# Adding softmax weights of two key blocks on GpSimd before the product with ones, and moving the normalisation's transfers

## The chip, the cores and the metric

The kernel runs on one core of a Trainium2 chip. The metric is the time of one execution on the device in microseconds (us). The core has a matrix engine (TensorE, PE in the profile), VectorE (DVE), ScalarE (ACT), GpSimd (POOL) and SyncE (SP); each works through its own instruction list in order, and semaphores tie the lists together. SP issues most of the DMA transfers, POOL some.

## The reference, cut to what matters

```python
h = layernorm(x) * (1 + ca) + sa
q, k, v = projections of layernorm(h), 16 heads of 32; q, k rotated, then layernormed per head
scores = einsum('bhqd,bhkd->bhqk', q, k) / sqrt(32)
scores = where(causal, scores, min)
w = softmax(scores, axis=-1)
x = x + ga * (einsum('bhqk,bhkd->bhqd', w, v) @ Wo + bo)
x = x + gb * gated_ffn(layernorm(x) * (1 + cb) + sb)
```

Batch 4, 1024 positions, width 512, all in float32. Only the softmax and the product with V are touched here.

## The kernel before, in words

Four stages run one after the other: `qkv_stage`, `attention_stage` (L578), `project_stage`, `ffn_stage`. The change lies in `attention_stage` alone.

It works on 16 groups of four heads. Each engine's list is written out in steps `k`; a unit `n` is 12 consecutive steps, `w` is the step in the unit. In unit n the engines do, side by side: the scores of group n in natural orientation to find each row's maximum (`score` on PE L791, `peak` on DVE L877); the preparation of group n+1 in w=1 and w=3 (`prepare` on PE L782: eight transposes; `widen` on ACT L946; `high` on POOL L750: the part that float32r holds; `low` on DVE L872: the rest, `whole` minus `halves`, both in SBUF), after which SP copies the halves of four heads into `stack` (`lay_stacks`, L700, 12 transfers); and, 14 steps behind the scores, the softmax of a group by blocks: `BLOCKS` are the 12 pairs of a half of the queries and a block of 128 keys, with widths 512, 384, 256, 128 for the first half and 512 five times, 384, 256, 128 for the second.

For a block, `shift` (PE L812) makes scores minus maximum, transposed, for each of four heads, in one of two PSUM buffers (`psB`); `exponent` (ACT L953) writes `probT`; a step later `weigh` (PE L827) multiplies the four heads' `probT` with V into `psO`, and then again with a matrix of ones into `psL`, which gives the sums of the softmax. In step w, block w-2 is shifted and block w-3 weighed. After the last block of a half, `take` on DVE (L906) and ACT (L968) move `psO` and `psL` out.

The maxima: `gather` (DVE L894) makes a table from them at the end of w=11, with L897, L899, L902 and L904 in a row, each waiting for the one before; `turn_peaks` (PE L807) transposes it in w=0, ahead of that step's `weigh`; ACT copies it and SP lays it into the stack.

`normalise` (POOL L757) divides by the sums: they go out to DRAM (L759), come back as 128x32 (`few`, L761), DVE takes the reciprocal (L937), they go out again (L763) and come back over all partitions (L766, four transfers), and POOL multiplies (L769). POOL's queue issues these transfers and waits for each. SP's list in a unit: peaks in w=0, `load` and all 12 stack transfers in w=4, V in w=5, the store of group n-2 in w=10.

PE's order in a step is: shifts of heads 0 and 1, two score items, shifts of heads 2 and 3, then the transposes of a preparation or of the peaks where there are any, then `weigh` with V and with ones. A score item waits for the maximum of the item two before (two slots of `psA`).

## Time and profile before

| | us |
|---|---|
| median of 3 runs (lowest, highest) | 2434.78 (2433.34, 2436.04) |
| the profiled execution | 2436.47 |
| its span, first to last instruction | 2434.3 |
| PE, DVE, ACT, POOL busy | 2242.7, 1200.8, 792.2, 728.7 |
| attention stage, from its first load to its last store | 400 to 1208 |

Times in rows are us from the start of the span; a row of the timeline has start, duration, engine, line, operation, tile written <- tiles read, shape, and in brackets the idle time before it and what ended it. "PEld" is the load of weights into the matrix engine, "PE" the product itself; SPq and POOLq are instructions of a queue. Products are pipelined, so the start of the next one says more than the duration.

### The profile page before, as it was taken

The numbers are of one execution on the slowest core, as the hardware profiler recorded it, in microseconds if no ns is written. First come the engines' busy times: TensorE is split into PE (matmuls) and PEld (weight loads), VectorE is DVE, ScalarE is ACT, GpSimd is POOL, SyncE is SP. The second block draws the span as 40 slices with busy tenths as digits, with TensorE's granted clock in tenths as the row PEclk, the third lists the DMA queues.
The fourth block names the chain that finished last, engine by engine and source line by source line (L and its number), as shares of the span: only waits on it lengthen the run. The fifth ranks groups of instructions, "written<-read, shape, count | busy, mean of one in ns | idle before, by whom it ended". The sixth has DMA issues, their size and how long they took to land. (4 is left out here: it accounts for less than half of the span.)

```text
span 2434.3 us, 32672 instructions
## 1 busy us (share of the span) xinstructions
PE 2242.7 (92%) x12008; PEld 1649.6 (68%) x12008; DVE 1200.8 (49%) x2775; ACT 792.2 (33%) x1671; POOL 728.7 (30%) x694
## 2 busy tenths in 40 slices
PE   6999993799999999999678799999999999999998
PEld 3777771455555555555356588888888888888887
DVE  5999995566665665665279512222222222221212
ACT  3333331155555555555445411111111111111111
POOL 2677775002112112111277122222222222222221
PEclk8999996599999999999899899999999999999999
DMA  6222223555465465452288411212121211111111
GB/s 225 70 96 94 103 87 120 118 134 132 102 152 126 107 151 130 107 128 76 68 256 303 161 52 52 70 48 69 52 69 49 66 56 65 52 64 37 52 53 52
DMA packets 161834, 243.71 MB, mean 100 GB/s; under 512 B 17124, under 2 KB 84292, under 8 KB 161184
## 3 DMA queue, kind: packets, MB, share of 16 engines
q1 hardware_dynamic: 153184, 220.66, 31.0%
q0 software_dynamic: 7456, 18.07, 2.6%
q10 hardware_dynamic: 1056, 3.15, 0.3%
q8 instruction: 87, 1.43, 0.2%
q14 instruction: 51, 0.42, 0.1%
HBM read 131.69 MB, written 59.26 MB: 78 GB/s over the span
## 5 line engine op out<-in xcount | busy, mean ns | idle before, releaser
L1324 DVE TENSOR_TENSOR f_gu<-f_psU,f_silu 128x512 f32<-128x512 f32 x128 | 88.6, 692 | 712.3 <-PE f_psU L1391 712.3
L961 ACT ACTIVATE b_probT<-b_psB 128x512 f32<-128x512 f32 (+3 forms) x768 | 339.4, 490 | 300.0 <-PE b_psB L824 220.9
L891 DVE TENSOR_REDUCE b_top<-b_psA 128x2 f32<-128x1024 f32 (+2 forms) x320 | 288.6, 902 | 134.0 <-PE b_psA L803 133.8
L1280 POOL TENSOR_SCALAR f_wd_hi<-f_wd 128x512 fp32r<-128x512 f32 x128 | 83.4, 652 | 819.7 <-PE f_psD L1376 775.9
L821 PE MATMUL b_psB<-b_stack 98*128 98x512 f32 (+3 forms) x768 | 273.6, 401 | 5.1 <-ACT b_probT L961 4.6
L821 PEld LDWEIGHTS b_psB<-b_stack 98*128 98x128 f32 x768 | 141.4, 189 | 156.0 <-issue 103.2
L1300 ACT ACTIVATE f_silu<-f_psG 128x512 f32<-128x512 f32 x128 | 76.5, 598 | 504.2 <-PE f_psG L1391 504.2
L803 PE MATMUL b_psA<-b_stack 96*128 96x512 f32 (+3 forms) x768 | 193.5, 373 | 35.8 <-DMA b_stack<-b_halves 20.1
L1389 PE MATMUL f_psG<-f_hT_hi,w_hi 128*128 128x512 f32 x512 | 200.4, 391 | 11.0 <-DVE f_hT_lo L1318 11.0
L1391 PE MATMUL f_psG<-f_hT_lo,w_hi 128*128 128x512 f32 x512 | 199.9, 390 | 0.0
L1390 PE MATMUL f_psG<-f_hT_hi,w_lo 128*128 128x512 f32 x512 | 199.9, 390 | 0.0
L1295 ACT ACTIVATE f_gu_hi<-f_gu 128x512 fp32r<-128x512 f32 x128 | 80.9, 632 | 364.5 <-DVE f_gu L1324 364.5
L1390 PE MATMUL f_psU<-f_hT_hi,w_lo 128*128 128x512 f32 x512 | 199.2, 389 | 0.0
L1391 PE MATMUL f_psU<-f_hT_lo,w_hi 128*128 128x512 f32 x512 | 199.2, 389 | 0.0
L1389 PE MATMUL f_psU<-f_hT_hi,w_hi 128*128 128x512 f32 x512 | 199.2, 389 | 0.0
L1374 PE MATMUL f_psD<-f_wd_hi,f_gu_hi 128*128 128x512 f32 x512 | 199.2, 389 | 0.0
L1375 PE MATMUL f_psD<-f_wd_lo,f_gu_hi 128*128 128x512 f32 x512 | 199.2, 389 | 0.0
L1376 PE MATMUL f_psD<-f_wd_hi,f_gu_lo 128*128 128x512 f32 x512 | 199.2, 389 | 0.0
L803 PEld LDWEIGHTS b_psA<-b_stack 96*128 96x128 f32 x768 | 136.2, 200 | 65.9 <-issue 22.6
L1282 POOL TENSOR_TENSOR f_wd_lo<-f_wd,f_wd_hi 128x512 fp32r<-128x512 f32 x128 | 168.8, 1319 | 10.7
L839 PE MATMUL b_psO<-b_probT,b_v 128*32 128x512 f32 (+3 forms) x1536 | 165.4, 503 | 0.0
L839 PE MATMUL b_psL<-b_probT,b_ones 128*32 128x512 f32 (+3 forms) x1536 | 159.0, 486 | 0.0
(178 smaller groups left out, 4084.4 us busy)
## 6 DMA issues: line engine op xcount, KB each, us to landing
b_stack<-b_halves SPq DMA_DIRECT2D x192, 256.0 KB, 5.1
f_wd<-in_wd_t SPq DMA_DIRECT2D x128, 256.0 KB, 2.6
qkv_d<-a_t SPq DMA_DIRECT2D x32, 512.0 KB, 2.7
b_land<-qkv_d SPq DMA_DIRECT2D x32, 512.0 KB, 4.7
a_x<-in_x SPq DMA_DIRECT2D x32, 256.0 KB, 3.3
qkv_d<-a_v SPq DMA_DIRECT2D x32, 256.0 KB, 3.1
b_v<-qkv_d SPq DMA_DIRECT2D x16, 512.0 KB, 5.8
att_d<-b_att SPq DMA_DIRECT2D x16, 512.0 KB, 3.2
```

The lines of the kernel that those rows point to most:

```text
L803: mm = pe.matmul(out[:, h, 0:hi - lo], stack[0:ROWS, n % BUFS, 1, j, t * P:(t + 1) * P], stack[0:ROWS, n % BUFS, 0, j, lo:hi], start=True, ...
L821: mm = pe.matmul(psB[:, i % 2, cols], stack[0:NR, n % BUFS, 0, j, kb * P:(kb + 1) * P], stack[0:NR, n % BUFS, 1, j, first * P:(half + 1) * ...
L839: mm = pe.matmul(out[rows, (first - half * HALF) * P:W], ones[:] if summing else v[:, n % 2, kb, rows], probT[:, (NW * n + w) % 3, j, 0:(h ...
L891: last = dve.tensor_reduce(into, tile[:, :, 0:width], AX.X, ALU.max, negate=True)
L961: act.activation(probT[:, (NW * n + w) % 3, j, 0:width], psB[:, i % 2, 0:width], ACT.Exp).then_inc(s["expd"], 1)
L1282: pool.tensor_tensor(wd_lo[:, u % 2], wd[:, u % 2], wd_hi[:, u % 2].bitcast(F32), ALU.subtract).then_inc(s["wd_lo"], 1)
L1374: pe.matmul(out_t, gu_hi[:, u % 2, cols], wd_hi[:, u % 2], start=first, stop=False)
L1375: pe.matmul(out_t, gu_hi[:, u % 2, cols], wd_lo[:, u % 2], start=False, stop=False)
L1376: mm = pe.matmul(out_t, gu_lo[:, u % 2, cols], wd_hi[:, u % 2], start=False, stop=end)
L1389: pe.matmul(out_c, w_hi[:, m, k, cols], hi, start=(k == 0), stop=False)
L1390: pe.matmul(out_c, w_lo[:, m, k, cols], hi, start=False, stop=False)
L1391: mm = pe.matmul(out_c, w_hi[:, m, k, cols], lo, start=False, stop=(k == KC - 1))
```

## The change

It does four things. (1) `add_pair` on POOL adds the exponents of two neighbouring key blocks in place, head by head (four additions per pair, as wide as the second block), and PE multiplies with ones once per pair (`add_up`), three steps after the pair's second shift, in even steps only. (2) `probT` has five buffers in place of three. (3) SP lays the stack of one head (three transfers) per step, in w=4 to 7. (4) The transfers of the normalisation move from POOL's list to SP's, in w=6, 7, 9 and 10; DVE takes the reciprocal in w=8 as before, POOL multiplies in two halves in w=11, and the store goes to w=2 of the next unit.

```diff
...
     BUFS = 3
+    PROBS = 5
 
...
         return (at[0], BLOCKS[at[1]][0]) if at and BLOCKS[at[1]][1] == (BLOCKS[at[1]][0] + 1) * HALF - 1 else None
+
+    def pair_at(k):
+        at = shift_at(k)
+        return (at[0], at[1] // 2) if at and at[1] % 2 == 1 else None
+
+    def sum_at(k):
+        return pair_at(k - 3)
+
+    def take_sum_at(k):
+        return take_at(k - 2)
 
...
         peak_rows = sb("b_peak_rows", [8 * TB, P])
-        probT = sb("b_probT", [P, 3, 4, W])
+        probT = sb("b_probT", [P, PROBS, 4, W])
         sums = sb("b_sums", [P, 2, C])
...
 
-            def lay_stacks(n):
-                at_least(sp, s["shifted"], 4 * NW * (n - BUFS + 1))
-                sp.wait_ge(s["lo_done"], 2 * n + 2)
-                for j in range(4):
-                    for r, pair in enumerate((slice(0, 4, 3), slice(2, 4), slice(0, 2))):
-                        sp.dma_start(stack[r * HD:(r + 1) * HD, n % BUFS, :, j].bitcast(F32),
-                                     halves[j * HD:(j + 1) * HD, pair].bitcast(F32)).then_inc(stack_in[j], 16)
+            def lay_stacks(n, j):
+                if j == 0:
+                    at_least(sp, s["shifted"], 4 * NW * (n - BUFS + 1))
+                    sp.wait_ge(s["lo_done"], 2 * n + 2)
+                for r, pair in enumerate((slice(0, 4, 3), slice(2, 4), slice(0, 2))):
+                    sp.dma_start(stack[r * HD:(r + 1) * HD, n % BUFS, :, j].bitcast(F32),
+                                 halves[j * HD:(j + 1) * HD, pair].bitcast(F32)).then_inc(stack_in[j], 16)
 
...
                 sp.dma_start(dst, att[:, n % 2].rearrange("p (t q) -> p t q", q=P)).then_inc(stored, 16)
+
+            def sums_out(n):
+                sp.wait_ge(s["taken_l"], 2 * n + 2)
+                sp.dma_start(scratch["sums"][0], sums[0:P:HD, n % 2]).then_inc(s["sums_out"], 16)
+
+            def few_in(n):
+                sp.wait_ge(s["sums_out"], 16 * n + 16)
+                sp.dma_start(few[:, 0], scratch["sums"][0].rearrange("j (a c) -> (j a) c", c=C // HD)).then_inc(s["few_in"], 16)
+
+            def few_out(n):
+                sp.wait_ge(s["inverted"], n + 1)
+                sp.dma_start(scratch["sums"][1].rearrange("j (a c) -> (j a) c", c=C // HD), few[:, 1]).then_inc(s["few_out"], 16)
+
+            def wide_in(n):
+                sp.wait_ge(s["few_out"], 16 * n + 16)
+                for j in range(4):
+                    sp.dma_start(sums[j * HD:(j + 1) * HD, n % 2], scratch["sums"][1, j:j + 1].broadcast_to([HD, C])).then_inc(s["wide_in"], 16)
 
...
                     load(n + 2)
-                if w == 4 and n + 1 < NG:
-                    lay_stacks(n + 1)
-                if w == 5 and 0 <= n < NG:
+                if 0 <= n - 2 < NG - 1 and w in (6, 7, 9, 10):
+                    {6: sums_out, 7: few_in, 9: few_out, 10: wide_in}[w](n - 2)
+                if 4 <= w < 8 and n + 1 < NG:
+                    lay_stacks(n + 1, w - 4)
+                if w == 7 and 0 <= n < NG:
                     load_v(n)
-                if w == 10 and 0 <= n - 2 < NG:
-                    store(n - 2)
+                if w == 2 and 0 <= n - 3 < NG:
+                    store(n - 3)
             sp.wait_ge(stored, 16 * NG)
...
 
+            def add_pair(n, i):
+                half, kb = BLOCKS[2 * i + 1]
+                width = (half + 1) * W - max(kb, half * HALF) * P
+                at = (NW * n + 2 * i) % PROBS
+                whole_at = (half + 1) * W - max(kb - 1, half * HALF) * P
+                pool.wait_ge(s["weighed"], NW * n + 2 * i + 1)
+                for j in range(4):
+                    into = probT[:, at, j, whole_at - width:whole_at]
+                    pool.wait_ge(s["expd"], 4 * (NW * n + 2 * i + 1) + j + 1)
+                    add = pool.tensor_tensor(into, into, probT[:, (at + 1) % PROBS, j, 0:width], ALU.add)
+                add.then_inc(s["added"], 1)
+
             def normalise(n):
-                pool.wait_ge(s["taken_l"], 2 * n + 2)
-                pool.dma_start(scratch["sums"][0], sums[0:P:HD, n % 2]).then_inc(s["sums_out"], 16)
-                pool.wait_ge(s["sums_out"], 16 * n + 16)
-                pool.dma_start(few[:, 0], scratch["sums"][0].rearrange("j (a c) -> (j a) c", c=C // HD)).then_inc(s["few_in"], 16)
-                pool.wait_ge(s["inverted"], n + 1)
-                pool.dma_start(scratch["sums"][1].rearrange("j (a c) -> (j a) c", c=C // HD), few[:, 1]).then_inc(s["few_out"], 16)
-                pool.wait_ge(s["few_out"], 16 * n + 16)
-                for j in range(4):
-                    pool.dma_start(sums[j * HD:(j + 1) * HD, n % 2], scratch["sums"][1, j:j + 1].broadcast_to([HD, C])).then_inc(s["wide_in"], 16)
                 pool.wait_ge(s["wide_in"], 64 * n + 64)
                 pool.wait_ge(s["taken_o"], 2 * n + 2)
-                pool.tensor_tensor(att[:, n % 2], att[:, n % 2], sums[:, n % 2], ALU.mult).then_inc(s["scaled"], 1)
+                for half in range(2):
+                    cols = slice(half * W, (half + 1) * W)
+                    mul = pool.tensor_tensor(att[:, n % 2, cols], att[:, n % 2, cols], sums[:, n % 2, cols], ALU.mult)
+                mul.then_inc(s["scaled"], 1)
 
...
                     high(*prep_at(k))
-                at = take_at(k)
-                if at and at[1] == 1 and at[0] < NG - 1:
-                    normalise(at[0])
+                if pair_at(k):
+                    add_pair(*pair_at(k))
+                n, w = unit(k)
+                if w == 11 and 0 <= n - 2 < NG - 1:
+                    normalise(n - 2)
 
...
 
-            def weigh(n, w, summing):
+            def weigh(n, w):
                 half, kb = BLOCKS[w]
-                if not summing:
-                    pe.wait_ge(s["expd"], 4 * (NW * n + w) + 4)
-                    if w == 0:
-                        pe.wait_ge(s["v_in"], 16 * n + 16)
+                pe.wait_ge(s["expd"], 4 * (NW * n + w) + 4)
+                if w == 0:
+                    pe.wait_ge(s["v_in"], 16 * n + 16)
                 if kb == 0:
-                    at_least(pe, s["taken_l" if summing else "taken_o"], 2 * n + half)
+                    at_least(pe, s["taken_o"], 2 * n + half)
                 first = max(kb, half * HALF)
-                out = psL if summing else psO
                 for j in range(4):
                     rows = slice(j * HD, (j + 1) * HD)
-                    mm = pe.matmul(out[rows, (first - half * HALF) * P:W], ones[:] if summing else v[:, n % 2, kb, rows],
-                                   probT[:, (NW * n + w) % 3, j, 0:(half + 1) * W - first * P],
+                    mm = pe.matmul(psO[rows, (first - half * HALF) * P:W], v[:, n % 2, kb, rows],
+                                   probT[:, (NW * n + w) % PROBS, j, 0:(half + 1) * W - first * P],
                                    start=(kb == 0), stop=(kb == (half + 1) * HALF - 1), skip_group_check=True)
-                mm.then_inc(s["summed" if summing else "weighed"], 1)
+                mm.then_inc(s["weighed"], 1)
+
+            def add_up(n, i):
+                half, kb = BLOCKS[2 * i]
+                pe.wait_ge(s["added"], NW // 2 * n + i + 1)
+                if kb == 0:
+                    at_least(pe, s["taken_l"], 2 * n + half)
+                first = max(kb, half * HALF)
+                for j in range(4):
+                    mm = pe.matmul(psL[j * HD:(j + 1) * HD, (first - half * HALF) * P:W], ones[:],
+                                   probT[:, (NW * n + 2 * i) % PROBS, j, 0:(half + 1) * W - first * P],
+                                   start=(kb == 0), stop=(kb == (half + 1) * HALF - 2), skip_group_check=True)
+                mm.then_inc(s["summed"], 1)
 
...
                 if weigh_at(k):
-                    weigh(*weigh_at(k), False)
-                    weigh(*weigh_at(k), True)
+                    weigh(*weigh_at(k))
+                if sum_at(k):
+                    add_up(*sum_at(k))
 
...
                     low(*prep_at(k))
-                at = take_at(k - 5)
-                if at and at[1] == 1 and at[0] < NG - 1:
-                    dve.wait_ge(s["few_in"], 16 * at[0] + 16)
+                n, w = unit(k)
+                if w == 8 and 0 <= n - 2 < NG - 1:
+                    dve.wait_ge(s["few_in"], 16 * (n - 2) + 16)
                     dve.reciprocal(few[:, 1], few[:, 0]).then_inc(s["inverted"], 1)
-                at = take_at(k)
+                at = take_sum_at(k)
                 if at and at[0] == NG - 1:
...
                 if j == 0:
-                    at_least(act, s["summed"], NW * n + w - 2)
-                    at_least(act, s["weighed"], NW * n + w - 2)
+                    before = NW * n + w - PROBS
+                    if before % 2 == 0:
+                        at_least(act, s["summed"], before // 2 + 1)
+                    else:
+                        at_least(act, s["added"], before // 2 + 1)
+                        at_least(act, s["weighed"], before + 1)
                 width = (half + 1) * W - max(kb, half * HALF) * P
-                act.activation(probT[:, (NW * n + w) % 3, j, 0:width], psB[:, i % 2, 0:width], ACT.Exp).then_inc(s["expd"], 1)
+                act.activation(probT[:, (NW * n + w) % PROBS, j, 0:width], psB[:, i % 2, 0:width], ACT.Exp).then_inc(s["expd"], 1)
 
...
             def take(n, half):
-                act.wait_ge(s["summed"], NW * n + (HALF if half == 0 else NW))
+                act.wait_ge(s["summed"], (NW * n + (HALF if half == 0 else NW)) // 2)
                 at_least(act, s["scaled"], n - 1)
...
                         exponent(*shift_at(k), j)
-                    if j == 1 and take_at(k):
-                        take(*take_at(k))
+                    if j == 1 and take_sum_at(k):
+                        take(*take_sum_at(k))
                 if prep_at(k):
...
```

## Rows read from the trace of the kernel before

**Rows 1.** The page, busy time of the engines: us, share of the span, instructions.

```profile
PE 2242.7 (92%) x12008; PEld 1649.6 (68%) x12008; DVE 1200.8 (49%) x2775; ACT 792.2 (33%) x1671; POOL 728.7 (30%) x694
```

**Rows 2.** Busy time in a stretch: PE, PEld, DVE, ACT, POOL, clock, DMA share, GB/s.

```profile
616.00:664.00 48.00, 46.22 (x362) 27.71 (x360) 30.89 (x98) 26.37 (x57) 8.13 (x10) 1.00 0.51 123
```

**Rows 3.** The timeline, transposition of the peaks in w=0 of two units.

```profile
699.64 0.14 PEld L810 LDWEIGHTS b_psA<-b_ident,b_peaks 128*128 128x128 f32 x1
...
745.34 0.14 PEld L810 LDWEIGHTS b_psA<-b_ident,b_peaks 128*128 128x128 f32 x1
```

**Rows 4.** The timeline, step w=8 and the start of w=9, PE alone.

```profile
727.57 0.73 PE L821 MATMUL b_psB<-b_stack 98*128 98x512 f32 x2
...
729.67 1.06 PE L839 MATMUL b_psO<-b_probT,b_v 128*32 128x512 f32 x8
...
730.56 1.04 PE L839 MATMUL b_psL<-b_probT,b_ones 128*32 128x512 f32 x8
...
731.53 0.50 PE L821 MATMUL b_psB<-b_stack 98*128 98x512 f32 x1
```

**Rows 5.** The timeline, the two preparations in w=1 and w=3.

```profile
703.69 1.06 PE L788 MATMUL b_psA<-b_ident,b_land 128*128 128x128 f32 x8 [0.44 <-DVE b_top L891]
...
707.23 1.22 DVE L875 TENSOR_TENSOR b_halves<-b_whole,b_halves 128x1024 fp32r<-128x1024 f32 x1 [2.39 <-POOL b_halves L755]
...
714.27 1.05 POOL L755 TENSOR_SCALAR b_halves<-b_whole 128x1024 fp32r<-128x1024 f32 x1 [7.08 <-ACT b_whole L950]
...
715.35 1.23 DVE L875 TENSOR_TENSOR b_halves<-b_whole,b_halves 128x1024 fp32r<-128x1024 f32 x1 [2.86 <-POOL b_halves L755]
```

**Rows 6.** The timeline, start of w=1, and ones at width 256 with the next step.

```profile
701.33 0.33 PE L821 MATMUL b_psB<-b_stack 98*128 98x128 f32 x1
...
720.39 0.61 PE L839 MATMUL b_psL<-b_probT,b_ones 128*32 128x256 f32 x8
...
720.93 0.73 PE L821 MATMUL b_psB<-b_stack 98*128 98x512 f32 x2
```

**Rows 7.** The timeline, w=11, the gather of the peaks and the start of w=0.

```profile
739.69 0.44 PE L821 MATMUL b_psB<-b_stack 98*128 98x384 f32 x1
...
742.80 1.04 PE L839 MATMUL b_psL<-b_probT,b_ones 128*32 128x512 f32 x8
743.58 0.19 DVE L897 TENSOR_TENSOR b_least<-b_top 128x32 f32<-128x32 f32 x1
...
743.77 0.39 PE L821 MATMUL b_psB<-b_stack 98*128 98x256 f32 x1
...
744.25 0.19 DVE L904 TENSOR_TENSOR b_peaks<-b_least,b_peaks 128x32 fp32r<-128x32 f32 x1
```

**Rows 8.** Groups by line and shape: busy us, mean ns, idle before and its releaser.

```profile
L769 POOL TENSOR_TENSOR b_att<-b_att,b_sums 128x1024 f32<-128x1024 f32 x15 | 35.7, 2382 | 39.5 <-DMA b_sums<-sums_d 39.5
L273 POOL TENSOR_TENSOR a_h<-a_h,mod 128x512 f32<-128x512 f32 x32 | 41.0, 1280 | 0.0
```

**Rows 9.** The timeline, DVE beside POOL in the first and third stage.

```profile
75.42 1.92 POOL L281 TENSOR_TENSOR a_t<-a_t,a_hmean 128x1024 f32<-128x1024 f32 x1
...
76.56 0.81 DVE L407 TENSOR_SCALAR a_den<-a_vsum,a_ms2h 128x32 f32<-128x32 f32 x1
...
1235.00 1.28 POOL L1094 TENSOR_TENSOR w_lo<-p_wland,w_hi 128x512 fp32r<-128x512 f32 x1
1235.15 1.69 DVE L1150 TENSOR_TENSOR p_x<-p_gated,p_x 128x512 f32<-128x512 f32 x1
...
1240.55 0.69 DVE L1150 TENSOR_TENSOR p_x<-p_gated,p_x 128x512 f32<-128x512 f32 x1
```

**Rows 10.** Stacks seven to nine; landing of L759 (sums) and L761 (few), 568 to 1144.

```profile
723.94 3.37 SPq L705 DMA_DIRECT2D b_stack<-b_halves  x3
...
DMA to landing us min/median/max: 1.9/3.1/7.1
...
DMA to landing us min/median/max: 1.9/3.9/5.4
```

More of the change, by code:

```diff
@@ L665, in attention_stage @@
         names = ("mask_in ln_ready whole ident_ready consts k_ones qk_in v_in turned hi_done lo_done scored maxed peaks_ready "
-                 "peaks_turned peaks_copied peaks_in shifted expd weighed summed taken_o taken_l sums_out few_in inverted few_out "
+                 "peaks_turned peaks_copied peaks_in shifted expd weighed added summed taken_o taken_l sums_out few_in inverted few_out "
                  "wide_in scaled end_inverted end_scaled").split()
```

## The prediction

> **What bounds the kernel now.** I read the page's totals first: TensorE (PE) is busy for 92% of the span, VectorE (DVE) for 49%, GpSimd (POOL) for 30% [rows 1]. The change touches only the attention stage, so the table by stretches comes next: in 48 us of its middle PE is busy for 46.22 at a granted clock of 1.00 (the 2.4 GHz level), DVE for 30.89, ScalarE (ACT) for 26.37 and POOL for 8.13 [rows 2]. PE looks like the bound with a lot of free POOL beside it. That is an average, so I looked at one unit (12 steps, w = 0 to 11) step by step in the timeline. The transposition of the peaks, once per unit in w=0, starts at 699.64 and again at 745.34 [rows 3]: a unit takes 45.70 us, and 15 of them make up most of the stage.
>
> Two kinds of steps are to be seen. In w=7 to 11, PE sets the pace: step w=8 starts at 727.57, the products with V at 729.67, those with ones at 730.56, the next step at 731.53 [rows 4]. The 2.10 us before V are a ping-pong with ACT through two PSUM buffers (the third and fourth shift wait for exponents); 0.89 us are V, 0.97 us ones. In w=1 to 3, a chain sets the pace: transposes on PE at 703.69, ACT's widening, POOL's high part, DVE's low part at 707.23, then the maxima, scores and transposes queued behind it, and once more high at 714.27 and low at 715.35 [rows 5]. DVE stood idle for 2.39 and 2.86 us before its low parts, for POOL's high part, and PE's products with ones lie beside that chain at no cost. After it, DVE has maxima to catch up until w=6.
>
> **The products with ones.** A set costs 0.97 us at width 512 [rows 4] and 0.54 at 256 (720.39 to 720.93 [rows 6]), so 0.43 per 256 columns: 0.76 at 384 and 0.33 at 128. A unit has 6, 2, 2 and 2 of these: 5.82 + 1.52 + 1.08 + 0.66 = 9.08 us. Afterwards six sets are left, all in even steps: 4 x 0.97 + 2 x 0.54 = 4.96. So 4.12 us of PE work per unit go, 66 us in 16 units. What of it shows is a sum along the path, from the end of the second low part (T0 = 715.35 + 1.23 = 716.58 [rows 5]):
> - T0 to w=11: 23.11 us now (739.69 [rows 7]). w=4 to 6 win nothing: DVE's queued maxima set them, and w=6 gets a 512 set for a 128 one. w=7 and w=9 lose their sets of 512: 0.89 each, not 0.97, since V's set then bears the drain before the next step. w=8 has 256 in place of 512, 0.43. w=10 is unchanged. 23.11 - 0.89 - 0.43 - 0.89 = 20.9.
> - w=11: 4.08 - 0.89 = 3.19, and from there 1.57 to the peaks (743.77 to 745.34 [rows 3, 7]): 4.76 in place of 5.65.
> - Peaks to w=1: 1.69 (699.64 to 701.33 [rows 3, 6]), plus 0.21 for 512 in place of 384: 1.90.
> - w=1 to T0: 15.25 now (701.33 to 716.58 [rows 5, 6]), the chain: nothing won there, and the 512 set that w=2 gets lies beside it.
> Without any new wait a unit would take 20.9 + 4.76 + 1.90 + 15.25 = 42.8 us, 2.9 less.
>
> **What POOL takes over.** Its tensor_tensor takes 2382 ns for 1024 columns and 1280 ns for 512 [rows 8], so about 2.15 ns per column and 0.18 fixed: 1.0 us at 384 and 0.46 at 128. Per unit there are 4 x (1.0 + 0.46 + 1.28 + 1.28 + 1.0 + 0.46) = 22 us of additions, 2.6 for the scaling in halves and 2.1 for the two high parts: 27 of 43 us. Each pair is needed three steps later (some 9 us) and takes at most 5.1, so as an engine POOL isn't the bound, and its high parts come before the additions of their step.
>
> **What those additions do to DVE** is where I leave the intended sum. In the stage after attention, DVE's L1150 reads two SBUF tiles of 512 columns. When it is first (1240.55) it takes 0.69; started at 1235.15, 0.15 us behind a POOL operation that ran until 1236.28, it took 1.69 and ended 0.56 us after POOL did [rows 9]. A tensor_scalar of 128x32 (L407) took 0.81 us and ended at 77.37, right behind POOL's 75.42 + 1.92 = 77.34 [rows 9]. So such a DVE operation waits for the POOL operation under way. Before, POOL was mostly idle in attention; now three places meet:
> - First low part (two SBUF operands, 707.23, woken by the high part's end): behind that high part POOL's next instruction is an addition of 128 columns, its operands long ready. I take POOL as first: until 707.65, then DVE's 1.1 us of columns: +0.3 us on the chain.
> - Second low part, the same with 384 columns: 715.32 + 1.02, then 1.1: +0.9 us.
> - The gather of the peaks: L897, L899, L902, L904, 0.19 each, at 743.58 to 744.44, from 3.89 us after the start of w=11 [rows 7]. POOL's additions of pair 4 wait for block 8's product with V, which ends 3.11 us after that same start (742.80), so they run from about 3.25 to 7.35, four in a row. Each gather operation waits for its own predecessor, and meanwhile POOL has started its next: they end with additions 1, 2, 3, 4, at 7.35 in place of 4.75. The peaks' transposition stands in PE's queue ahead of V and ones; its turn now comes at 4.76, so all of it is stall: 7.45 in place of 4.76, +2.7 us.
> The bounds of each: nothing if DVE gets in first, and one whole addition per operation above; I take what the order of the two queues gives.
> No row shows the cast L902 beside POOL; the nearest is L407, which was held. The Trainium skill, "SBUF — State Buffer", section "Who interferes with whom", says that copies and casts can take the shared port pair as well as operations with two SBUF inputs; by that all four wait, while with a free cast the gather would end one addition (1.0 us) earlier. The nearest row alone gives the same choice.
>
> Unit: 20.9 + 7.45 + 1.90 + 15.25 + 1.2 = 46.7 us, **1.0 us longer than now**.
>
> **Normalisation on SyncE's queue (SP).** The reciprocal on DVE in w=8 now waits for a transfer that left POOL's queue for SP's. SP issues six stack transfers from T0 on (the seventh now starts at 723.94), then the sums, three more stacks (now 723.94 + 3.37 = 727.31, so 727.9 with the sums before them), then `few`, 128x32. With the medians of POOL's transfers (sums 3.1, `few` 3.9) it lands at 727.9 + 3.9 = 731.8, T0 + 15.2; with the slowest (7.1 and 5.4) at 723.94 + 12.5 = 736.4, T0 + 19.8 [rows 10]. From landing to w=11: reciprocal 0.35, maxima of w=9 1.23 + 0.84, scores to the third shift 0.45, the rest of w=10 2.76 (this unit's own spacing), together 5.6. Behind the wait stand the maxima of w=9, and for those PE's scores of w=10. So it costs nothing up to T0 + 15.3, and beyond, 1 us per us. I take 15.2, the medians: nothing, with thin cover. The later steps (four broadcasts, scaling on POOL) have some 3 us to spare before the next high part; POOL loses seven issues and their waits, SP gets them. Nothing waits behind SP's other new places: the stacks are needed 12 us later, V's tile later still. The Trainium skill, "DMA: Bandwidth & Descriptors", section "Queues, rings and completion order", has each DMA engine take one ring's descriptors in order; by that `few` waits behind the stacks issued before it; the sum stays if that wait fits into the 3.9 us, and each us more would be one of C. No row here shows it.
>
> **The sum.** Units 2 to 14: 13 x 1.0 = +13.0. Unit 1 (first low part free): +0.7. Unit 15 (no low parts, so all odd steps win; gather held): -1.1. The last unit has no scores, wins 3 and pays 2 at the end for four last additions and their set: -1. Total +11.6. The profiled execution took 2436.47 us (span 2434.3), 1.7 above the median of the runs, 2434.78. Against that median: **2446 us**.
>
> **Rivals.**
> A, the forecast, 0.50: own range 2434 to 2460.
> B, the gather slips through (faster), 0.22: if the additions are over or not yet begun when DVE gathers, the 2.7 us go and a unit takes 44.0; with free low parts as well 42.8. 15 units: 25 to 43 us off, 2392 to 2410. It decides at one point, whether a POOL addition runs 3.9 us after w=11 starts. For it: PE's 66 us of removed work are real. Against: both sides hang on the same PE step.
> C, `few` lands late and DVE stands in w=8 (slower still), 0.20: with a landing at T0 + 17.3, about midway between the two ends, +2 us in 13 units: 2472. For: twelve stacks fill that stretch, and the sums once took 7.1. Against: the medians.
> D, only part of the gather is held, or one low part gets in first, 0.08: about 0.9 us less per unit: 2434.
>
> **Numbers.** Differences under 0.2% (4.9 us) can't be told from none for this kernel. Below 2408 lies about a tenth (the better half of B), above 2478 less than a tenth (C beyond its middle). Faster: B and a sliver of A and D, 0.25; same: D and the lower edge of A, 0.09; slower 0.66.
>
> **What would show it.** The transpositions of the peaks 46 to 47 us apart; L897 to L904 taking some 0.3 to 1.0 us each and ending with POOL's additions; PE idle before L810's counterpart, released by DVE's peaks; the second low part near 2 us in place of 1.23; products with ones 80 to 90 us busy in place of 159; no idle DVE before the reciprocal. The forecast is wrong if the gather keeps 0.19 per operation (B), or if the reciprocal waits for `few` (C).

## The result, and the profile after

After: 2497.03 us, median of 4 runs (2494.32 to 2499.82); before, beside it, 2434.15 (2433.34 to 2436.04). The ratio is 1.0253, 95% interval 1.0240 to 1.0266: slower, as forecast, but by 63 us in place of some 11, and outside the range of 2434 to 2460. The profiled execution took 2494.82 us, its span is 2492.8 (before 2434.3).

The page of the kernel after, its busy times (us, share of the span, instructions), to be held against [rows 1]:

```profile
PE 2241.2 (90%) x11240; PEld 1644.5 (66%) x11240; DVE 1250.1 (50%) x2775; ACT 793.5 (32%) x1671; POOL 1040.3 (42%) x988
```

768 products fewer, and PE is as long busy as before (2242.7): what is left of its work runs slower. POOL has 312 us more, DVE 49 us more with the same number of instructions.

The timeline of the kernel after, one unit: the transposition of the peaks at both ends, the start of w=1, both low parts, the start of w=11 ([rows 3, 5, 6, 7] before):

```profile
723.54 0.18 PEld L848 LDWEIGHTS b_psA<-b_ident,b_peaks 128*128 128x128 f32 x1 [3.13 <-DVE b_peaks L953]
...
726.98 0.33 PE L859 MATMUL b_psB<-b_stack 98*128 98x128 f32 x1
...
732.88 1.48 DVE L924 TENSOR_TENSOR b_halves<-b_whole,b_halves 128x1024 fp32r<-128x1024 f32 x1 [2.40 <-POOL b_halves L785]
...
741.25 2.02 DVE L924 TENSOR_TENSOR b_halves<-b_whole,b_halves 128x1024 fp32r<-128x1024 f32 x1 [2.86 <-POOL b_halves L785]
...
764.36 0.44 PE L859 MATMUL b_psB<-b_stack 98*128 98x384 f32 x1
...
772.20 0.18 PEld L848 LDWEIGHTS b_psA<-b_ident,b_peaks 128*128 128x128 f32 x1 [3.12 <-DVE b_peaks L953]
```

This unit takes 48.66 us, one of three so short; the other ten between 520.06 and 1174.35 take 50.5 to 51.3 us, and the mean is (1174.35 - 520.06) / 13 = 50.33, against 45.70 in [rows 3]. In front of each transposition PE now stands idle for some 3.1 us and waits for DVE's table of the peaks. Why that is late, the same timeline shows a few us earlier:

```profile
767.76 3.86 POOL L796 TENSOR_TENSOR b_probT<-b_probT 128x384 f32<-128x384 f32 x4 [2.39 <-PE b_psO L875]
...
768.25 0.57 DVE L946 TENSOR_TENSOR b_least<-b_top 128x32 f32<-128x32 f32 x1
...
768.85 0.92 DVE L948 SCALAR_TENSOR_TENSOR b_least<-b_corner,b_least 128x32 f32<-128x32 f32 x1
769.80 0.90 DVE L951 CAST b_peaks<-b_least 128x32 fp32r<-128x32 f32 x1
770.74 0.92 DVE L953 TENSOR_TENSOR b_peaks<-b_least,b_peaks 128x32 fp32r<-128x32 f32 x1
771.58 2.50 POOL L804 TENSOR_TENSOR b_att<-b_att,b_sums 128x512 f32<-128x512 f32 x2
```

Four operations of 0.19 us each [rows 7] take 0.57 to 0.92 and end one by one with POOL's four additions (0.965 us each from 767.76). The cast is among them, as the Trainium skill ("SBUF — State Buffer", "Who interferes with whom") allows for casts: it takes 0.90 us here and 0.18 with POOL idle. DVE's work on the maxima, which reads PSUM, isn't held: between 468 and 1270 us its reductions of 128x1024 take 1219 ns on average, 1223 in the kernel before. The 49 us that DVE gained lie in the gather and in the low parts.

What I had not looked for stands in the column of the granted clock, behind the five columns of busy time. The table by stretches of the kernel after, behind the transposition at 772.20, then behind the second preparation of two units (columns as in [rows 2]):

```profile
770.00:772.00 2.00, 0.00 (x0) 0.00 (x0) 1.97 (x5) 0.00 (x0) 2.00 (x3) 0.80 0.00 0
772.00:774.00 2.00, 1.77 (x13) 0.69 (x17) 0.85 (x7) 0.27 (x1) 2.00 (x2) 0.50 0.01 4
774.00:776.00 2.00, 2.00 (x13) 0.34 (x6) 0.00 (x0) 0.00 (x0) 0.07 (x1) 0.50 0.38 104
776.00:778.00 2.00, 2.00 (x8) 1.90 (x9) 0.34 (x3) 0.56 (x2) 0.00 (x0) 0.50 0.62 175
778.00:780.00 2.00, 2.00 (x11) 1.90 (x10) 2.00 (x8) 0.56 (x2) 0.00 (x0) 0.50 0.00 0
780.00:782.00 2.00, 2.00 (x14) 1.04 (x13) 0.06 (x1) 0.95 (x1) 0.00 (x0) 0.64 0.00 0
...
692.50:694.50 2.00, 0.86 (x3) 0.43 (x4) 2.00 (x7) 0.66 (x2) 2.00 (x3) 1.00 0.54 112
...
696.50:698.50 2.00, 2.00 (x8) 1.57 (x6) 1.20 (x10) 1.11 (x3) 1.37 (x4) 0.50 0.97 201
...
743.50:745.50 2.00, 0.75 (x3) 0.32 (x3) 2.00 (x7) 0.77 (x3) 2.00 (x3) 1.00 0.71 171
745.50:747.50 2.00, 2.00 (x16) 1.39 (x17) 2.00 (x6) 0.50 (x2) 0.75 (x2) 1.00 0.98 203
```

The clock starts to fall in the last us of the stall (0.80 in the first row, in which PE does nothing). Behind the stall PE runs at 0.50, the 1.2 GHz level; a set of V's products of width 384 takes 1.51 us at 772.61, 0.85 at full clock. From the same view in stretches of 1 us I made a strip for each unit of the kernel after, one sign per us for the first 42 us from the transposition on: the clock in tenths, a dot for 1.00 (rounded). Three kinds of unit are there (13 between 520.06 and 1174.35):

```
start   unit
723.54  48.66  5559......................................   3 units
772.20  50.58  5555555559................................   5 units
672.51  51.03  555....................85555558...........   5 units
```

Every unit has the **first fall**, 3 to 4 us or 8 to 10 us long, behind the stall. Five also have a **second fall** of some 7 us. It follows a gap behind the late second low part, where PE waits for DVE's maxima and is busy for 0.86 of 2 us at 692.5. The short unit has the same gap (0.75 at 743.5) and no fall behind it. What decides among the three kinds I can't tell from the rows. A long first fall costs 1.9 us more than a short one, a second fall 2.4.

The groups of the kernel after, POOL by shape and PE's products with ones, and one line of its waits between 568 and 1200 (the last line: us in total, times, longest):

```profile
L796 POOL TENSOR_TENSOR b_probT<-b_probT 128x512 f32<-128x512 f32 x128 | 160.5, 1284 | 115.5 <-PE b_psO L875 115.5
L796 POOL TENSOR_TENSOR b_probT<-b_probT 128x384 f32<-128x384 f32 x128 | 137.5, 1103 | 47.1 <-PE b_psO L875 47.1
L796 POOL TENSOR_TENSOR b_probT<-b_probT 128x128 f32<-128x128 f32 x128 | 67.2, 555 | 26.7 <-PE b_psO L875 26.7
...
L887 PE MATMUL b_psL<-b_probT,b_ones 128*32 128x512 f32 (+1 forms) x768 | 102.7, 611 | 1.9 <-POOL b_probT L796 1.9
...
DVE b_few L986 <- DMA b_few<-sums_d: 7.4, 7, 2.1
```

PE hardly ever waits for the additions (1.9 us in all). DVE's reciprocal waits 7.4 us in total for `few`; the longest of these waits, 2.1 us at 959.89, lies in a unit of 48.69 us, as short as the others of its kind. So the work moved to POOL and to SP is in time, and the cost is beside it. The products with ones are busy for 102.7 us, where the prediction had 80 to 90: some of them run at half clock.

### The profile page after: what moved, and what is told of

The parts are those of the page before. It is cut to its first block and busy times, and to the rows that moved or that the text cites. A ratio compares the mean times of both kernels' runs of the same rounds, so it can differ in the third digit from the quotient of the medians.

```text
span 2492.8 us, 31660 instructions
## 1 busy us (share of the span) xinstructions
PE 2241.2 (90%) x11240; PEld 1644.5 (66%) x11240; DVE 1250.1 (50%) x2775; ACT 793.5 (32%) x1671; POOL 1040.3 (42%) x988
## 5 line engine op out<-in xcount | busy, mean ns | idle before, releaser
L796 POOL TENSOR_TENSOR b_probT<-b_probT 128x128 f32<-128x128 f32 (+2 forms) x384 | 365.3, 981 | 189.4 <-PE b_psO L875 189.4
L859 PE MATMUL b_psB<-b_stack 98*128 98x512 f32 (+3 forms) x768 | 282.0, 414 | 5.1 <-ACT b_probT L1014 4.6
L859 PEld LDWEIGHTS b_psB<-b_stack 98*128 98x128 f32 x768 | 146.5, 198 | 183.0 <-ACT b_probT L1014 97.3
L841 PE MATMUL b_psA<-b_stack 96*128 96x512 f32 (+3 forms) x768 | 205.5, 389 | 53.2 <-DVE b_top L940 31.8
L841 PEld LDWEIGHTS b_psA<-b_stack 96*128 96x128 f32 x768 | 142.7, 211 | 91.7 <-DVE b_top L940 47.9
L937 DVE CUSTOM_DVE_ANT_0 b_masked<-b_psA,b_mask 128x128 f32<-128x128 f32 x512 | 124.5, 283 | 105.4 <-PE b_psA L841 105.2
L875 PE MATMUL b_psO<-b_probT,b_v 128*32 128x512 f32 (+3 forms) x1536 | 175.8, 533 | 0.0
```

What stands on the lines that cost most here:

```text
L796: add = pool.tensor_tensor(into, into, probT[:, (at + 1) % PROBS, j, 0:width], ALU.add)
L841: mm = pe.matmul(out[:, h, 0:hi - lo], stack[0:ROWS, n % BUFS, 1, j, t * P:(t + 1) * P], stack[0:ROWS, n % BUFS, 0, j, lo:hi], start=True, ...
L859: mm = pe.matmul(psB[:, i % 2, cols], stack[0:NR, n % BUFS, 0, j, kb * P:(kb + 1) * P], stack[0:NR, n % BUFS, 1, j, first * P:(half + 1) * ...
L875: mm = pe.matmul(psO[rows, (first - half * HALF) * P:W], v[:, n % 2, kb, rows], probT[:, (NW * n + w) % PROBS, j, 0:(half + 1) * W - first ...
```

## The experiments

Each kernel was timed against the kernel before, at 2435 to 2437 us. A "unit" is the distance of two transpositions of the peaks, the "wait" is PE's idle time in front of one. Three theories are named: **H**, DVE is held by POOL's operations under way; **S**, the transfers moved to SP cost time; and the clock, that PE's half speed behind a stall costs time beyond the stall. The expectations name a rival to the last, **T**: the clock falls because PE has less work in the stage, whatever the stall. The kernel after and the first three experiments make a table of two by two: with and without each kind of guard, a wait that makes POOL's additions start later.

**Gather guarded.** The additions of pair 4 wait until the peaks' table is done; nothing else is changed.

```diff
                 pool.wait_ge(s["weighed"], NW * n + 2 * i + 1)
+                if i == 4 and n + 1 < NG:
+                    pool.wait_ge(s["peaks_ready"], 4 * (n + 2))
```

> Changed kernel, but POOL starts the four additions of pair 4 only after DVE's gather of the peaks. Theory H (the additions hold the gather, PE stands idle for 3.1 us per unit in front of the peaks, and its clock falls behind that stall): both go, a unit takes 20.9 + 4.8 + 1.9 + 16.4 = 44.0 us in place of 50.3 on average, total 2497 - 15 x 6.3 = about 2403, granted clock in the stage near 1.00. Rival T (the clock falls because PE has less work in the stage, whatever the stall): only the 3.1 us go, about 2450, clock still near 0.9. Rival S (the time comes from the transfers on SP's queue): unchanged, 2497.

Measured: 2423.75 us (2422.99 to 2428.15), ratio 0.9957 (0.9941 to 0.9974). The timeline of this kernel:

```profile
786.08 0.19 DVE L948 TENSOR_TENSOR b_least<-b_top 128x32 f32<-128x32 f32 x1
...
786.53 0.18 DVE L953 CAST b_peaks<-b_least 128x32 fp32r<-128x32 f32 x1
...
787.08 3.90 POOL L798 TENSOR_TENSOR b_probT<-b_probT 128x384 f32<-128x384 f32 x4 [3.88 <-DVE b_peaks L955]
...
787.50 0.14 PEld L850 LDWEIGHTS b_psA<-b_ident,b_peaks 128*128 128x128 f32 x1 [0.58 <-DVE b_peaks L955]
```

The gather is back at 0.19 per operation, the wait at 0.58, and a unit takes 44.57 us; three of 13 take 47.0 to 47.3, with the second fall alone, some 22 us behind the transposition. One wait, which delays POOL's pair 4 by 1.5 us in each unit, takes 73 us off. Theory T had 2450 here and is off by 26 us. Theory H had 2403 with units of 44.0: the measured time is 21 us above that, since a unit is 0.57 longer (most of it the time from the table to the transposition, see below) and the second fall stays in three.

**Low parts guarded.** The additions in w=1 and w=3 wait for the low half of their step; the gather stays unguarded.

```diff
                 if pair_at(k):
+                    if prep_at(k):
+                        pool.wait_ge(s["lo_done"], 2 * prep_at(k)[0] + prep_at(k)[1] + 1)
                     add_pair(*pair_at(k))
```

> Changed kernel, but in w=1 and w=3 POOL's additions wait for DVE's low part; the gather stays held. Theory H: the low parts take 1.22 us again, the chain of w=1 to 3 is 0.3 + 0.8 us shorter, 13 or 14 units: about 2482; the 3.1 us in front of the peaks and the clock stay. If the low parts' hold lay beside other work: 2497.

Measured: 2467.92 us (2466.09 to 2469.50), ratio 1.0135 (1.0118 to 1.0152). The low parts take 1.22 and 1.23 us again, the wait stays at 3.13, and the units take 47.7 us each, nearly all within 0.3 us. Behind the stalls the clock falls in every unit, but for 4 us only (7 in the first of the 13, which takes 48.69), and there is no second fall. The expectation had left all the falls in place; it was 14 us too high.

**Both guards.** The two diffs above together.

> Both guards, gather and low parts. Theory H: 42.8 to 43.1 us per unit, about 2388, faster than both kernels by some 2% and 4%. Rival T: 2435. Rival S: 2497.

Measured: 2399.01 us (2395.51 to 2400.58), ratio 0.9845 (0.9829 to 0.9861). The timeline of this kernel:

```profile
732.28 0.14 PEld L852 LDWEIGHTS b_psA<-b_ident,b_peaks 128*128 128x128 f32 x1 [0.59 <-DVE b_peaks L957]
...
734.18 0.33 PE L863 MATMUL b_psB<-b_stack 98*128 98x128 f32 x1
...
748.20 1.23 DVE L928 TENSOR_TENSOR b_halves<-b_whole,b_halves 128x1024 fp32r<-128x1024 f32 x1 [2.86 <-POOL b_halves L785]
...
770.51 0.44 PE L863 MATMUL b_psB<-b_stack 98*128 98x384 f32 x1
...
775.81 0.14 PEld L852 LDWEIGHTS b_psA<-b_ident,b_peaks 128*128 128x128 f32 x1 [0.59 <-DVE b_peaks L957]
```

A unit takes 43.53 us, and in none of the 13 does the clock fall, with as few products as in the kernel after: that leaves nothing of T, which had 2435. The time is 11 us above what H said (2388, with units of 42.8 to 43.1). This is the unit without any hold, part by part: 1.90 to w=1, 15.25 to the end of the second low part (749.43), 21.08 to w=11, 5.30 to the peaks. The table, in us per unit, with the mean of 13 units:

| | low parts guarded | not guarded |
|---|---|---|
| gather guarded | 43.54, mean 43.56 | 44.57 (3 of 13: 47.0 to 47.3), mean 45.16 |
| not guarded | 47.7, mean 47.81 | 48.66 where it is short, mean 50.33 |

By the means the hold of the low parts alone costs 1.60 us (1.03 of it without the second falls), that of the gather 4.25, and the two together 6.77, 0.9 more than their sum. By the medians of the whole executions it is 25, 69 and 98 us, 4 more than the sum. The strips show where the 0.9 lies: with both holds there are five long first falls and five second ones, with the gather's hold alone none of either kind from 565.05 on, and with that of the low parts alone three second falls.

The low parts hold POOL in turn: from the kernel after to the one with both guards, the mean of its additions of 384 columns falls from 1103 to 1004 ns and that of 128 columns from 555 to 455. At 512 columns, in steps without a low part, it stays (1284 and 1288).

**A late turn.** PE transposes the peaks after the products of w=0, so that 1.9 us of work cover part of the wait; no guards.

```diff
-                if peaks_at(k) is not None:
-                    turn_peaks(peaks_at(k))
                 if weigh_at(k):
...
                     add_up(*sum_at(k))
+                if peaks_at(k) is not None:
+                    turn_peaks(peaks_at(k))
```

> Changed kernel, but PE transposes the peaks behind the step's products with V and ones in place of ahead of them; the gather is held as before. Theory H: 1.7 to 1.9 us of products fill part of the 3.1 us, about 1.3 us of idle PE are left; if such a short stall costs no clock a unit takes 48.7 - 1.5 - 1.8 = 45.4, total about 2423; if any stall costs it, about 2465. Rival T: the clock stays near 0.9 however the stall is filled, about 2468. Rival S: 2497.

Measured: 2463.97 us (2454.60 to 2468.93), ratio 1.0109 (1.0082 to 1.0135). The wait is still up to 2.3 us (31.3 in total, 14 times), the units take 46.4 to 48.9. The clock still falls behind it (0.50 from 714.4 to 716.4), but in eight of 13 units only, and nine have the second fall. H with a price for any stall (2465) and T (2468) both fit the time; this run doesn't part them. Moving the waiting instruction helps less than moving what it waits for.

**Transfers alone.** The kernel before, with SP's order and the normalisation of the kernel after; products with ones, buffers and POOL's free time as before.

```diff
-                if w == 4 and n + 1 < NG:
-                    lay_stacks(n + 1)
...
+                if 0 <= n - 2 < NG - 1 and w in (6, 7, 9, 10):
+                    {6: sums_out, 7: few_in, 9: few_out, 10: wide_in}[w](n - 2)
+                if 4 <= w < 8 and n + 1 < NG:
+                    lay_stacks(n + 1, w - 4)
```

> The kernel before with only the second half of the change: stacks laid one head per step, the normalisation's transfers on SP, the scaling in two halves, the store in w=2; products with ones per block, no additions. Theory H (the whole loss comes from the additions holding DVE, and the clock behind it): 2435 within 5 us, since the wait for few is short and no PE work changes; if few comes late it may add up to 1 us per unit, 2450. Rival S: most of the loss, 2480 or more.

Measured: 2434.86 us (median of 10 runs), ratio 1.0000 (0.9991 to 1.0010); unit 45.70, but for two of 47.3, as in the kernel before. Theory S falls: in the kernel before, this half of the change costs nothing and gives nothing.

**A late table in the kernel before.** No additions on POOL, but a spare reciprocal on DVE in the gather, of 600 columns in one kernel and of 300 in the other: the stall by itself.

```diff
...
+                dve.reciprocal(spare[:, 1, 0:600], spare[:, 0, 0:600])
                 dve.wait_ge(s["peaks_ready"], 4 * n + 3)
...
```

> The kernel before, with a reciprocal of 128x600 elements of a spare tile (some 3.9 us, its result unused) put into DVE's gather before its last operation: PE then stands in front of the peaks for about 3.0 us with no addition on POOL anywhere. Theory H, clock part (an idle PE of 3 us lets the granted clock fall, and the products behind it run at 1.2 GHz): a unit grows by 3.0 plus 1.5 to 3.5, from 45.7 to 50.2 to 52.2, total 2505 to 2535, granted clock in the stage 0.9 to 0.96. Rival (the clock falls for another cause, such as POOL's activity or fewer products): only the 3.0 us, 48.7 per unit, 2480, clock 0.99 or 1.00.

> The kernel before with a reciprocal of 128x300 added on VectorE ahead of the peaks' transposition, half the width of the run whose unit rose from 45.7 to 51.3 us. By the width the reciprocal takes about 2 us. If the clock falls only behind the longer stall, a unit rises by the stall alone, about 1.5 to 2.0 us, and the time to 2458 to 2466 us, with the granted clock of the attention near 0.97. If a stall of this length too brings the clock down, some 1.5 to 3.5 us a unit come on top: 2480 to 2515 us.

Measured with 600: 2524.53 us (2523.77 to 2527.71), ratio 1.0365 (1.0348 to 1.0383). With 300: 2466.28 us (2463.32 to 2472.45), ratio 1.0125 (1.0108 to 1.0143). The timeline and the table by stretches of the kernel with 600 columns:

```profile
775.71 3.90 DVE L905 RECIPROCAL b_spare<-b_spare 128x600 f32<-128x600 f32 x1
...
780.18 0.14 PEld L811 LDWEIGHTS b_psA<-b_ident,b_peaks 128*128 128x128 f32 x1 [3.33 <-DVE b_peaks L907]
```

```profile
780.00:782.00 2.00, 1.79 (x17) 0.56 (x17) 0.82 (x7) 0.27 (x1) 0.00 (x0) 0.83 0.00 0
782.00:784.00 2.00, 2.00 (x11) 1.67 (x8) 0.00 (x0) 0.56 (x2) 0.00 (x0) 0.50 0.07 16
784.00:786.00 2.00, 2.00 (x9) 1.81 (x9) 1.77 (x10) 0.45 (x2) 0.00 (x0) 0.50 0.00 0
786.00:788.00 2.00, 2.00 (x16) 1.44 (x18) 0.63 (x1) 0.49 (x2) 0.00 (x0) 0.50 0.03 8
```

and of the kernel with 300 columns:

```profile
756.94 2.02 DVE L905 RECIPROCAL b_spare<-b_spare 128x300 f32<-128x300 f32 x1
...
759.54 0.14 PEld L811 LDWEIGHTS b_psA<-b_ident,b_peaks 128*128 128x128 f32 x1 [1.46 <-DVE b_peaks L907]
```

```profile
760.00:762.00 2.00, 2.00 (x22) 1.04 (x15) 0.18 (x1) 0.47 (x3) 0.00 (x0) 1.00 0.04 8
762.00:764.00 2.00, 1.56 (x12) 1.36 (x11) 1.68 (x10) 0.70 (x3) 0.00 (x0) 1.00 0.04 8
```

With 2.02 us more on DVE the wait is 1.46 and most units take 47.10, 1.40 more than 45.70. The table is done at 759.01, 6.51 us after the start of w=11 (752.50), in place of 4.75: it is 1.76 later, and PE used to come some 0.36 later than the table allowed. In ten of 13 units the clock stays at 1.00 throughout. In one it falls for 4 us behind the wait (48.73 us), in two there and once more 13 us later (50.3). With 3.90 the same rule gives 45.70 + 1.40 + 1.88 = 48.98, yet the units take 50.6 to 52.2, mostly 51.2 to 51.5, with a fall of 4 to 9 us behind every wait. So a stall of 3.3 us costs about 2.3 us beyond itself here. No POOL addition and no moved product are needed for that. The kernel with 300 columns shows the price of a fall without a change of the stall: with the same wait of 1.46 a unit takes 47.10 without a fall, 48.73 with one of 4 us, and 50.3 with two.

**The wait filled.** The kernel after, with nine spare products of 512 columns on PE ahead of the transposition, into the two PSUM buffers `psB`, which are overwritten next.

```diff
+            def fill(g, b):
+                pe.wait_ge(s["expd"], 4 * (NW * g + b) + 4)
+                for i in range(9):
+                    pe.matmul(psB[:, i % 2, :], stack[0:ROWS, g % BUFS, 1, 0, 0:P],
+                              stack[0:ROWS, g % BUFS, 0, 0, 0:W], start=True, stop=True)
...
+                if peaks_at(k) is not None and shift_at(k):
+                    fill(*shift_at(k))
                 if peaks_at(k) is not None:
                     turn_peaks(peaks_at(k))
```

> Changed kernel; while PE would stand in front of the peaks it computes nine products of 512 columns into the PSUM buffer that the exponents have left (result unused, about 1.9 us), so the gather is held as before but PE is idle for only about 1 us. Theory H: same place of the peaks in the unit, but no fall of the clock: 50.3 - 3.3 = 47.1 per unit on average, about 2449, granted clock near 1.00. Rival T (clock falls whatever fills the stall): 2497.

Measured: 2472.88 us (2466.19 to 2482.77), ratio 1.0160 (1.0127 to 1.0193), 24 us faster than the kernel after, by work that nobody needs; T had 2497. The table comes exactly as late (its four operations take 0.57 to 0.94 us), but PE's wait is 0.65. None of the 13 units has a fall behind its transposition, and six of them take 47.2, as against 48.66: even a short first fall costs 1.5 us. The other seven take 48.0 to 49.9. Six of these have the second fall, which the expectation of 2449 had left out; here is one of them, behind the gap at 732:

```profile
732.00:736.00 4.00, 2.72 (x16) 2.00 (x12) 4.00 (x11) 1.12 (x4) 3.25 (x3) 0.89 0.69 157
736.00:740.00 4.00, 4.00 (x18) 2.34 (x17) 2.24 (x12) 1.77 (x5) 1.69 (x4) 0.50 0.97 201
```

**Additions of one column.** The additions are cut to a single column each, so the sums leave out the rest of every second block.

```diff
-                    into = probT[:, at, j, whole_at - width:whole_at]
+                    into = probT[:, at, j, whole_at - 1:whole_at]
...
-                    add = pool.tensor_tensor(into, into, probT[:, (at + 1) % PROBS, j, 0:width], ALU.add)
+                    add = pool.tensor_tensor(into, into, probT[:, (at + 1) % PROBS, j, width - 1:width], ALU.add)
```

> Changed kernel, each addition on POOL cut to its last column, so POOL's instructions, waits and the reduced number of products stay and only the time that POOL holds DVE goes (the sums leave out the second block of a pair but for one column; products and softmax sums are wrong for that reason). Theory H: 42.8 to 43.5 us per unit, the level that both guards reach or a little less: about 2390. Rival S: still above 2470.

Measured: 2454.08 us (2453.01 to 2457.09), ratio 1.0072 (1.0056 to 1.0089), far above the expectation. The timeline of this kernel tells why:

```profile
749.40 0.61 POOL L796 TENSOR_TENSOR b_probT<-b_probT 128x1 f32<-128x1 f32 x4 [6.80 <-PE b_psO L875]
749.89 0.19 DVE L946 TENSOR_TENSOR b_least<-b_top 128x32 f32<-128x32 f32 x1
749.96 2.49 POOL L804 TENSOR_TENSOR b_att<-b_att,b_sums 128x512 f32<-128x512 f32 x2
750.11 1.17 DVE L948 SCALAR_TENSOR_TENSOR b_least<-b_corner,b_least 128x32 f32<-128x32 f32 x1
751.32 1.17 DVE L951 CAST b_peaks<-b_least 128x32 fp32r<-128x32 f32 x1
752.52 0.19 DVE L953 TENSOR_TENSOR b_peaks<-b_least,b_peaks 128x32 fp32r<-128x32 f32 x1
```

With the additions out of the way, the scaling in two halves, next in POOL's list, starts under the gather, holds two of its operations for 1.17 us each, and the wait is 2.56. The experiment missed its aim, to take every hold away, but shows the hold with a second operation of POOL, the multiplication. L946, which began before the multiplication, took its 0.19 us, and the low parts take 1.23.

This kernel also gives the cleanest price of the clock. Two of its 13 units have no fall and take 45.51, which is 1.98 more than 43.53, the stall alone; one of them (896.08) begins behind the same wait of 2.56 as the rest. The other eleven, with a fall of 4 to 8 us behind the wait, take 47.1 to 48.1: 1.6 to 2.6 us more.

**Guards and a late turn.** The two guards, and the transposition behind the products of w=0 as in the diff of the late turn.

> GpSimd's additions of pair 4 wait for the peaks, those of steps w=1 and w=3 for the low halves, and PE turns the peaks after the eight matmuls of w=0, not before them. Hold theory: with the guards alone a unit took 43.54 us and the wait for the peaks about 0.6 us; that wait now lies beside matmuls, so a unit falls by up to 0.6 us, 15 times 9 us at most: 2391 to 2397 us. Rival, as the late turn showed without the guards (units uneven, the wait only partly covered): the peaks arrive later at the first step of the next unit, and the time is the same as with the guards, 2399 us, or above it.

Measured: 2393.94 us (2391.86 to 2396.62), ratio 0.9822 (0.9806 to 0.9838). The expectation of 2391 to 2397 held. The units take 42.86, with no fall of the clock in any of the 13, and nothing but PE's own order holds the transposition. This is the best version: 1.8% under the kernel before and 4.1% under the change as it was made.

## Why the prediction was right in its direction and wrong in its size

- **What PE wins** was right. Without holds the parts are 1.90, 15.25 and 21.08 (both guards) against 1.90, 15.25 and 20.9. The fourth, 4.76, is 5.30: 0.56 us pass between the end of the gather (775.25) and the transposition (775.81), the handover. It lay hidden in [rows 3, 7], where PE came 0.90 us after the table (744.44 to 745.34). Once PE comes earlier, it shows. That is a mis-sized term of about 0.5 us per unit.
- **The two low parts** were right: 1.48 and 2.02 us in place of 1.23 are +0.25 and +0.79, forecast +0.3 and +0.9. The guard takes 1.03 us off in units without a second fall.
- **The gather** was right in its mechanism and nearly in its size. It ended 7.30 us after the start of w=11 (771.66 - 764.36), forecast 7.35; PE went on at 7.84, forecast 7.45: the handover, 0.54 us here, had been taken as 0.1.
- **Rival B**, the gather slipping through, didn't come: PE waits for the table in each of the 13 units. The two queues hang on the same PE step, as its counter-argument said. Where guards make it true, both of its cases come out too low: with free low parts it had units of 42.8 and 2392 us, measured 2399.01 with both guards; with held ones 44.0 and 2410, measured 2423.75 with the gather guarded. The handover is some 8 us of each in 15 units, and the second falls in three units are some 7 us of the latter.
- **Rival C**, `few` landing late, didn't come. In the unit from 723.54 it was ready about 14.2 us after the second low part (forecast 15.2), its waits total 7.4 us and lengthen no unit, and the transfers alone give a ratio of 1.0000. Whether `few` waited behind the stacks in its ring no run told apart: its median to landing is 3.9 us, as in [rows 10].
- **The step that failed** is "so all of it is stall: 7.45 in place of 4.76, +2.7 us": the price of the stall. I took it one to one and kept every duration at the clock of 1.00 in [rows 2]. What the runs showed in its place: behind a stall of 3.1 us the clock falls, and a unit loses 1.5 to 3.9 us more at half clock, 3.2 on average, second falls included. In the short unit the parts are 3.44, 16.29, 21.09 and 7.84, together 48.66. Against the forecast 46.7 that is +1.54 (peaks to w=1, at half clock), -0.16, +0.19 and +0.39 (the handover). Long first falls and second falls in ten units of 13 add 1.67 on average, which makes 50.33, 3.63 over the forecast.

The sum over the stage: 13 x 3.63 = 47.2, less 3.3 for two units of the kernel before that were themselves longer than 45.70. The first and the last unit add 2.6 and 1.8, and behind the last transposition 1.3 are saved. That is 47.0; with the profiled execution of before and the forecast's 11.6 it gives 2436.5 + 11.6 + 47.0 = 2495.1 us, measured 2494.8. Of the 3.63 the clock is 1.54 + 1.67 = 3.2 and the rest the handover.

Could it have been seen? Yes: two units of the kernel before are 1.6 us longer than the others (745.34 to 792.67 is 47.33). Its table by stretches shows why:

```profile
757.00:759.00 2.00, 1.51 (x8) 1.51 (x8) 1.19 (x6) 0.45 (x2) 0.00 (x0) 0.65 0.00 0
759.00:761.00 2.00, 2.00 (x10) 0.40 (x12) 0.00 (x0) 1.21 (x1) 0.22 (x1) 0.50 0.07 19
```

A fall of 4 us stood in the trace, with its price, though behind a gap in the preparation and not behind the peaks. I had read the clock over one undisturbed stretch of 48 us, and set a range in which no case let it fall.

What stays open is why stalls and gaps of one length bring a fall of 4 us, of 9 us, or none, and why in these 13 units the second fall never follows a long first one. (In the first unit of the stage, from 468.57, both are there.) No run was made for that.

## What to carry to other kernels

Work moved to GpSimd isn't free where VectorE has short operations with their operands in SBUF on the critical chain. Here each of them waited out the GpSimd operation under way, so four of 0.19 us cost four additions of 0.965; VectorE's reductions out of PSUM were not held. Look for the places where both are woken by the same event, and make GpSimd wait for VectorE's chain; two such waits turned +2.5% into -1.5%. Price a new TensorE stall of about 3 us as the stall plus what follows at half clock, and look in the trace of before for units that are already longer than the rest.

## What the runs showed of the hardware that I had not expected

- Behind a PE stall of 3.1 to 3.3 us the granted clock is 0.50 for 3 to 10 us, in each of 13 units. With shorter stalls in front of the peaks it fell in eleven of 12 units at 2.56 us, in eight of 13 at 2.27 (the late turn), and in three of 13 at 1.46. Where spare products filled the stall it fell in none.
- Falls combine: behind the second low part the clock fell in 3 of 13 units without the gather's stall, in 5 with it, and in none once the low parts were free.
- The hold goes by operation, not by work: a cast of 128x32 took 0.90 us beside an addition of 384 columns, 1.17 beside a scaling of 512, and 0.18 alone. It goes both ways: POOL's additions of 384 columns took 1103 ns on average beside DVE's low parts, 1004 where they waited for them.
